# Row factors of a layer norm: copied by DMA from one SBUF partition to all 128, in place of spreading matmuls

## What is computed

```
h = x mixed over its 64 positions by a 64 x 64 matrix chosen per batch row
q, k = layernorm(silu(causal_conv4(h @ Wq or Wk)))       per head of 128 channels, 16 heads
v = h @ Wv ; beta = sigmoid(h @ Wb + bb) ; gate = silu(h @ Wg)
S_t = (1 - beta_t) S_(t-1) + beta_t v_t k_t ;  o_t = S_t q_t     over the positions of a row
x = x + (o * gate) @ Wo
x = x + ffn(adapter_dense(x))       int8-like rounding of rows, ternary weights
```

## Time and profile before

| | |
|---|---|
| median of 3 runs | 2813.45 us (2812.87 to 2815.73) |
| the profiled execution | 2813.33 us |
| its span | 2811.6 us |
| TensorE busy | 2592.2 us, 92% |
| VectorE, ScalarE, GpSimd busy | 60%, 43%, 25% |
| TensorE's granted clock, mean | 0.965 of full speed |
| DMA: bytes, mean rate | 416.17 MB, 148 GB/s |
| DMA: share of the 16 engines' span | 46.1% |

### The profile page before, as it was taken

One profiled execution on the slowest core, in us unless ns is written; L12 is line 12 of the kernel. 1 busy time (PEld: TensorE's weight loads), 2 busy tenths in 40 slices (PEclk: granted clock), 3 DMA queues, 4 the chain that ended last, 5 costly groups with the idle time before them and its releaser, 6 DMA issues.

```text
span 2811.6 us, 39966 instructions
## 1 busy us (share of the span) xinstructions
PE 2592.2 (92%) x14521; PEld 2009.7 (71%) x14536; DVE 1698.8 (60%) x2848; ACT 1195.0 (43%) x1878; POOL 694.7 (25%) x764
## 2 busy tenths in 40 slices
PE   3778889999999999999999999999999999999996
PEld 3556676777777677777777777776777777777764
DVE  4455555576666665656665666666656566656653
ACT  2444444444444444443444444444444534444431
POOL 1344442221222122222222221221222222222220
PEclk8889899999999999999999999999999999999998
DMA  4654554445443554534444454435544344444531
GB/s 132 192 186 152 168 195 144 145 133 172 156 152 110 164 182 128 163 110 160 161 151 141 133 167 158 150 113 170 175 140 151 121 159 161 144 141 131 165 98 45
DMA packets 264554, 416.17 MB, mean 148 GB/s; under 512 B 102058, under 2 KB 126634, under 8 KB 264362
## 3 DMA queue, kind: packets, MB, share of 16 engines
q1 hardware_dynamic: 264362, 413.63, 46.1%
HBM read 360.86 MB, written 52.69 MB: 147 GB/s over the span
## 4 chain that ended last, share of the span: by engine, by line
PE 83%; DVE 5%; ACT 4%; issue 3%; DMA 2%; POOL 1%; SPq 1%; DVEq 0%; ACTq 0%; POOLq 0%
PE ring L964 29%; PE pj_a L964 24%; PE pj_b L964 12%; PE ring L1178 4%; PE m L1168 2%; PE cen_q L1157 2%; PE var L1136 2%; PE cen_k L1157 1%; PE cen_k L1158 1%; PE cen_q L1158 1%; PE ring L1005 1%; ACT L886 1%; PE var L1147 1%; DVE r_parts L721 1%; PE ring L1084 1%
## 5 line engine op out<-in xcount | busy, mean ns | idle before, releaser
L700 DVE SCALAR_TENSOR_TENSOR y_q<-pj_a,conv,y_q 128x504 f32<-128x504 f32 (+2 forms) x384 | 281.7, 734 | 404.6 <-ACT y_q L881 395.5
L443 POOL TENSOR_TENSOR og_lo<-gt,og_hi 128x512 fp32r<-128x512 f32 x128 | 165.2, 1291 | 859.9 <-ACT og_hi L911 859.9
L964 PE MATMUL pj_a<-ht_hi,wg 128*128 128x512 f32 x1024 | 356.3, 409 | 2.0 <-DVE y_q L700 2.0
L964 PE MATMUL pj_a<-ht_hi,wq 128*128 128x512 f32 x1024 | 348.6, 402 | 2.8 <-DVE ht_lo L556 1.5
L964 PE MATMUL pj_b<-ht_hi,wk 128*128 128x512 f32 x1024 | 336.5, 389 | 8.4 <-DVE c_k L729 8.4
L964 PE MATMUL ring<-wo,og_hi 128*128 128x512 f32 x1024 | 321.0, 395 | 8.1 <-DMA wo<-parts_o 4.3
L964 PE MATMUL ring<-wv,ht_hi 128*128 128x512 f32 x1024 | 321.9, 395 | 0.0
L700 DVE SCALAR_TENSOR_TENSOR y_k<-pj_b,conv,y_k 128x504 f32<-128x504 f32 (+2 forms) x384 | 281.9, 734 | 63.5 <-ACT y_k L881 54.4
L869 ACT ACTIVATE sq_q<-cen_q 128x512 f32<-128x512 f32 x128 | 76.5, 598 | 441.9 <-PE cen_q L1158 441.9
L964 PEld LDWEIGHTS pj_a<-ht_hi,wq 128*128 128x128 f32 x1024 | 200.4, 196 | 48.8 <-issue 3.3
L964 PEld LDWEIGHTS ring<-wo,og_hi 128*128 128x128 f32 x1024 | 190.4, 189 | 62.2 <-issue 13.4
(11 more groups left out here) (206 smaller groups left out, 5136.7 us busy)
## 6 DMA issues: line engine op xcount, KB each, us to landing
wq<-parts_q SPq DMA_DIRECT2D x112, 512.0 KB, 3.7
wk<-parts_k SPq DMA_DIRECT2D x112, 512.0 KB, 4.4
wg<-parts_g SPq DMA_DIRECT2D x112, 512.0 KB, 3.5
wv<-parts_v SPq DMA_DIRECT2D x112, 512.0 KB, 6.3
wo<-parts_o SPq DMA_DIRECT2D x112, 512.0 KB, 5.6
keep<-keep_rows SPq DMA_DIRECT2D x256, 64.0 KB, 3.6
wo<-parts_w SPq DMA_DIRECT2D x32, 512.0 KB, 5.5
acc<-in_x_dram SPq DMA_DIRECT2D x8, 1024.0 KB, 6.7
```

The source lines that it names most:

```text
L443: G.tensor_tensor(og_lo[:, u % OG_RING, :], gt[:, u % GT_RING, :], og_hi[:, u % OG_RING, :].bitcast(F32), ALU.subtract).then_inc(S["oglo"], 1)
L700: V.scalar_tensor_tensor(out=yy[:, :, k:], in0=pp[:, :, :L - k], scalar=conv[:, i, h, 3 - k:4 - k], in1=yy[:, :, k:], op0=ALU.mult, op1=AL ...
L964: last = T.matmul(psum, a, b, start=start and n == 0 and m == 0, stop=stop and n == len(pairs) - 1 and m == 2)
```

## The change

- `rstd_hi`, `split_rstd` and `spread` are gone, with the tiles `r_parts`, `pick`, `is_low`, `signs`, seven small VectorE steps of the setup, and all waits on their semaphores (on the bank of k before its projection and on the banks of `cen` before `centre` among them).
- `load_rstd(m)` on SyncE waits for rr, then issues four DMAs: each copies one row of `rstd` (partition 0, 32, 64 or 96, 2 KB) to all 128 partitions of one of the four `sq` tiles (256 KB written). It stands in even slots between the load of `keep` and the load of the gate weights. `normalise` reads the tile from `sq` after waiting for that DMA.
- `squares`, which writes the `sq` tiles, now waits for normalise of two units before, in place of var.
- `variance` stands in front of the projection of k, `seed` in front of the first tap of k, `newton` between the taps of q and of k. `variance` waits for the newton of the pair before, `seed` for the four DMAs of the pair before.

```diff
+            def load_rstd(m):
+                sp.wait_ge(S["rr"], m + 1)
+                for j in range(4):
+                    x_ = "qk"[j % 2]
+                    row = rstd[32 * j:32 * j + 1, :].rearrange("p (o n) -> p o n", o=1)
+                    sp.dma_start(sq[x_][:, j // 2, :], row.broadcast_to([1, P, GROUP])).then_inc(S[f"r_in_{x_}{j // 2}"], 16)
...
+                if U % 2 == 0 and 2 <= U <= UNITS:
+                    load_rstd(U // 2 - 1)
                 if H <= U + 1 < UNITS:
                     load_head("g", U + 1)
...
-            def split_rstd(m):
-                dve.wait_ge(S["r_hi"], m + 1)
-                V.scalar_tensor_tensor(out=r_parts[:], in0=rstd[:], scalar=is_low[:], in1=r_parts[:].bitcast(F32),
-                                       op0=ALU.mult, op1=ALU.subtract).then_inc(S["r_split"], 1)
             def normalise(u):
                 for x_ in "qk":
-                    dve.wait_ge(S[f"bc_{x_}"], u + 1)
+                    dve.wait_ge(S[f"r_in_{x_}{u % 2}"], 16 * (u // 2 + 1))
                     dve.wait_ge(S[f"cc_{x_}"], u + 1)
                     c = c_[x_][:, u % C_RING, :]
-                    V.tensor_tensor(c, c, bc_banks[u % 2][x_][:], ALU.mult).then_inc(S[f"n_{x_}"], 1)
+                    V.tensor_tensor(c, c, sq[x_][:, u % 2, :], ALU.mult).then_inc(S[f"n_{x_}"], 1)
...
                     taps("q", U)
+                if U % 2 == 0 and 2 <= U <= UNITS:
+                    newton(U // 2 - 1)
+                if U < UNITS:
                     taps("k", U)
...
             def squares(x_, u):
                 act.wait_ge(S[f"cen_{x_}"], u + 1)
                 if u > 1:
-                    act.wait_ge(S["var"], u // 2)
+                    act.wait_ge(S[f"n_{x_}"], u - 1)
...
             def seed(m):
                 act.wait_ge(S["var"], m + 1)
                 if m:
-                    act.wait_ge(S["r_split"], m)
+                    for j in range(4):
+                        act.wait_ge(S[f"r_in_{'qk'[j % 2]}{j // 2}"], 16 * m)
...
                     gated_hi(U - 4)
+                if U % 2 == 0 and 2 <= U <= UNITS:
+                    seed(U // 2 - 1)
                 if U < UNITS:
                     first_tap("k", U)
...
                 elif x_ == "k" and u:
                     pe.wait_ge(S["tap_k"], 3 * u)
-                    if u % 2 and u > 2:
-                        pe.wait_ge(S["n_k"], u - 2)
...
                 if m:
-                    pe.wait_ge(S["n_q"], 2 * m - 1)
+                    pe.wait_ge(S["rr"], m)
...
                     project("q", U)
-                    project("k", U)
                 if U % 2 == 0 and 2 <= U <= UNITS:
                     variance(U // 2 - 1)
-                if U % 2 and 0 <= U - 2 < UNITS:
-                    spread(U - 2)
+                if U < UNITS:
+                    project("k", U)
...
-                if U % 2 == 0 and 2 <= U <= UNITS:
-                    spread(U - 2)
```

More of the change, by code:

```diff
@@ L112, in adaln_attn_ffn @@
         rstd = sb("rstd", [P, GROUP])
-        r_parts = sb("r_parts", [P, GROUP], F32R)
         keep = sb("keep", [P, 2, HALF])
@@ L135, in adaln_attn_ffn @@
         mean = sb("mean", [P, 32])
-        pick = sb("pick", [P, 4, P], F32R)
         conv = sb("conv", [P, 2, H, 5])
@@ L144, in adaln_attn_ffn @@
         eps_ln = sb("eps_ln", [P, 1])
-        is_low = sb("is_low", [P, 1])
-        signs = sb("signs", [P, 4, 1])
         st = sb("st", [P, 12, HT])
@@ L154, in adaln_attn_ffn @@
         pj = {"q": pj_a, "k": pj_b, "g": pj_a}
-        bc_banks = [{"q": var, "k": pj_b}, cen]
         w2_src = v
@@ L160, in adaln_attn_ffn @@
         junk = [gt[:, t, :] for t in range(KC)]
-        ones = sq["q"][:, 0, 0:P]
         SETUP_LOADS = 1 + KC + 4 + 4 + 1 + 2
-        SETUP_GAMMA, SETUP_TERN, SETUP_W2, SETUP_DVE = 26, 40, 48, 56
+        SETUP_GAMMA, SETUP_TERN, SETUP_W2, SETUP_DVE = 19, 33, 41, 49
         names = """setup_in dense_in subj_in wb_in gamma_out w2_out setup_pool setup_dve setup_act setup_pe
@@ L168, in adaln_attn_ffn @@
             w_hi_done w_split ring_mm0 ring_mm1 ring_free0 ring_free1
-            proj_q proj_k proj_g cen_q cen_k var scores bc_q bc_k weighed
+            proj_q proj_k proj_g cen_q cen_k var scores r_out r_in_q0 r_in_k0 r_in_q1 r_in_k1 weighed
             tap0_q tap0_k tap_q tap_k silu_q silu_k shi_q shi_k slo_q slo_k gated
-            sq_q sq_k cc_q cc_k seed newton_a newton_b rr r_hi r_split n_q n_k aff_q aff_k
+            sq_q sq_k cc_q cc_k seed newton_a newton_b rr n_q n_k aff_q aff_k
             scanned og_odd oghi oglo ht_hi beta_done keep_done x2_hi xam_mul xam_hi xam_lo ssq absmax small
@@ L502, in _ @@
                     step(V.tensor_copy(ident_in[half, t, :], ident[half, half]))
[L503 to L507, removed]
             dve.wait_ge(S["wb_in"], 16)
@@ L757, in _ @@
                 take(U, 0)
-                if U % 2 == 0 and 2 <= U <= UNITS:
-                    newton(U // 2 - 1)
                 if 0 <= U - 3 < UNITS:
@@ L763, in _ @@
                     silu_lo("k", U)
-                if U % 2 == 0 and 2 <= U <= UNITS:
-                    split_rstd(U // 2 - 1)
                 take(U, 1)
@@ L934, in _ @@
                     silu("q", U)
-                if U % 2 == 0 and 2 <= U <= UNITS:
-                    seed(U // 2 - 1)
                 take(U, 0)
@@ L942, in _ @@
                     silu("k", U)
-                if U % 2 == 0 and 2 <= U <= UNITS:
-                    rstd_hi(U // 2 - 1)
                 for b in blocks:
@@ L1137, in variance @@
                 mm.then_inc(S["var"], 1)
[L1139 to L1148, removed]
             def centre(x_, u):
@@ L1154, in centre @@
                     pe.wait_ge(S[f"sq_{x_}"], u)
-                if u % 2 and u > 2:
-                    pe.wait_ge(S[f"n_{x_}"], u - 1)
                 T.matmul(cen[x_][:], center[:], s_hi[x_][:], start=True, stop=False)
```

1 line of the change is left out of this document (removed).

## The result

The kernel after takes 4207.15 us (median of 4 runs, 4199.43 to 4210.32) against 2813.92 before in the same runs: a ratio of 1.494, 95% interval [1.492, 1.496]. The forecast was 4070 us in a range of 3200 to 4750, slower with a chance of 0.89.

The account below looks back on a forecast made before the run. TensorE, busy 92% of the span, was taken to bound the kernel. With the copies a pair's cycle becomes 60.7 us, 19.7 more than 41.0; 64 pairs add 1260 to 2813.3 us: 4070 us, range 3200 to 4750.

Parts of the forecast that it names:

- the added step: Four 256 KB DMAs per pair on SyncE behind rr, each from one partition, taking R = 10.2 us each.
- The end of 4.0 us: Lower bound for R, one copy's time: 256 KB from one DRAM row to 128 partitions landed in 4.0 us.
- The end of 51 us: Upper bound for R, one copy's time, from the keep_rows store: 5.1 GB/s per source partition.
- The cycle: Time from one rr to the next, per pair of slots: 19.7 + 4R = 60.7 us against 41.0 before.
- The removed step: Four spreading matmuls per pair on TensorE: 72 us, plus 23 us of waits for `r_parts`, if all else is hidden.
- the stall of 46.7 us: TensorE's 12 waits for `r_parts` in the steady part; half, 23 us, was counted as gained.
- the move: Variance ahead of k's projection, newton ahead of k's taps: costs nothing, covered by 1.4 us before the silu of k.
- The signs named ahead: Expected in the profile after: slow copies, waits for wg and sq, TensorE busy some 65%, DMA share 0.8 or more.
- The gain by R = 4 us: Rival 1: copies no slower than the row from DRAM, cycle 35.7 us, total 2718 us; chance 0.10.
- its threshold: The point from which the gain rival decides: 19.7 + 4R = 41.0, R = 5.3 us.
- rival 2: Moderate loss: the four copies overlap in part, effective R of 5.3 to 7.5, for instance 3114 us; chance 0.11.

Follow-up runs that it names:

- quarters: The kernel after with each of its four copies cut into four DMAs, each from 32 equal rows to 32 partitions: 2828.75 us, ratio to before 1.0046.

## Why the prediction was right

**The bound and the price of the added step** held: a copy was taken at 10.2 us from one engine's full rate; by itself it flows for 9.6 us. The number is better founded than its reason: that one source partition gives to all engines just what one engine moves at full rate was an assumption, and the rows of before held no copy that could show it. That it came so close is in part luck. The end of 4.0 us was the DRAM row's, and DRAM is just what makes the difference: over DRAM the copies do land in 3.6 and 4.6 us. The end of 51 us, the store's rate divided by its 16 partitions, was rightly left.

**The cycle.** I summed 60.7 us; later groups take 61.6 by their stores, an excess of 20.5 us against 19.7. From rr to rr their 55 cycles take 61.5 on average, but no single length: 47 take 53 to 63 us, and eight take 71 to 74. Inside, two errors offset each other. From rr to the start of the gate's projection: predicted 0.8 + 41.0 + 1.3 + 1.4 = 44.5, measured 41.7 on average and 2056.24 - 2017.25 = 39.0 in the cycle shown, because the fourth copy is there 37.6 us after the first issue (mean) and not 0.8 + 41.0: the copies overlap in part or lie below 10.2 us each. From there to the next rr: predicted 16.2, measured 19.8 on average and 2075.88 - 2056.24 = 19.6 in the cycle shown. Of its 3.4 us too many, the gate's projection took 4.8 us in place of 2.94 at a granted clock of 0.55, after TensorE had been idle, and the next weights of q came 1.2 us late. I had left the clock out of the sum. So the close agreement of 60.7 and 61.6 is luck in part: the two parts are off by about 3 us each, in opposite directions.

**The total.** 137 us were missing, 4 of them by rounding: 2813.3 + 64 x 19.7 is 4074. The step that was mis-sized is the 64 equal pairs. From rr to rr the first eight cycles take 595.4 us in place of 354.7, a loss of 240.7 where 8 x 19.7 is 158; the 55 later ones lose 1125 where the sum has 1084; and behind the last rr the kernel takes 119.0 us in place of 88.6, 30.4 where the sum has 19.7. Against that it reaches the first rr 3 us earlier. Together that is 133 us more than the sum, 83 of them in the first group. There the copies do not go out at rr. In six of its eight cycles they start 12 to 13 us behind it, since on SyncE they stand behind raw loads and saves that wait for splits of weights. In this one rr comes at 181.46 + 0.69 = 182.15 us (first VectorE's line, then SyncE's queue):

```profile
181.46 0.69 DVE L713 SCALAR_TENSOR_TENSOR rstd<-var,rstd 128x512 f32<-128x512 f32 x1
...
192.59 0.56 SPq L250 DMA_DIRECT2D parts_v<-wv  x1
193.19 0.61 SPq L258 DMA_DIRECT2D rows_b<-in_L_attn_Wg_dram  x1
193.84 1.68 SPq L287 DMA_DIRECT2D keep<-keep_rows  x2
195.57 0.61 SPq L295 DMA_DIRECT2D sq_q<-rstd  x1
```

The sum had 0.8 us from rr until bytes flow, from one slot of a later group.

**The removed step.** Predicted 72 + 23 = 95 us if all is hidden. Without copies the kernel gains 68, and the order takes 8.5 by itself, so removal is worth some 76, if the two add up. Of the stall of 46.7 us, 24.6 turned up at `s_lo_k`, which was next as said; if nothing of it went elsewhere, 22.1 us, about half, were really gained. That the move costs nothing was wrong by these 8.5 us in the first group, where my one slot from 1410 us could not show it.

**The signs named ahead.** Right: copies with landings far over 4 us, gate projections waiting for wg as TensorE's longest wait, normalise waiting for sq as VectorE's, TensorE busy 65%, stores of keep_rows 486 to 506 us apart behind the first group (570 in it) where I said 486. Too high: the DMA share, 0.74 and not 0.8. Not quite right: ScalarE loads tables 7 times more often ahead of silu (86 in place of 79); the run with the new order alone has 86 as well, so this comes from the order. Not foreseen: SyncE is held in the issue itself, for up to 13 us. I had said that the wait for rr delays no issue. That misses that the copies do.

**Rivals.** The gain by R = 4 us fell with the first profile. The runs over DRAM and with quarters show that it was wrong beyond its source: with copies that land in 2 to 5 us the loss is gone, as its threshold says, but the 2718 us are not reached (2817 and 2829). The rival took the order as free and left out what the copies and their issues cost in the first group. Copies that overlap were rival 2: in the kernel after they do so a little (37.6 us in place of 41.8), and even from four ports the time is 3524 us, above that rival's 3114 to 3370.

Not settled: why two copies on two ports by themselves overlap by only 2 us of 20.8 while four in the loaded queue overlap much more. The port rule alone does not give the first.

## What to carry to other kernels

Before a DMA broadcasts or gathers inside SBUF, count how many source partitions it reads and on which ports they lie, not only its bytes; 256 KB from one partition take 9.6 us here, a round trip by DRAM about 6 in all. If the value exists on 32 partitions anyway, reading all of them is quick too; here it took away the loss and brought no gain. A slow transfer costs more than its own consumer: price the loads that stand behind it in the same queue, and the clock that TensorE loses while it waits.

## What the runs showed that was not expected

- SyncE's issue of a DMA takes 0.6 us, but 7 to 10 us when some two slow copies are outstanding, and 13.1 at most.
- Moving the four source rows by 4, 8 and 12 partitions, with the same values and bytes, is worth 683 us (4207 to 3524).
- The DMA share of a profile says little of bytes: 0.92 stood beside 33 GB/s and 1.01 beside 410.
- Where the copies stand in the queue that issues DMAs is worth more in the first group than the matmuls removed: 45.8 and 43.0 us per pair with the same copies over DRAM placed in two ways, 2.8 us, where the four spreads took 1.13.
- The last copies cost more than their cycle: behind the last rr the kernel after takes 119.0 us, before 88.6.
